# Layer-1 attention scores of a two-layer block: two heads in the two 64-row halves of the array, six part products for eight, masks as 64-row pairs

## The reference

```python
# layer 0, per head
scores = jnp.einsum('bhqd,bhkd->bhqk', q, k) * scale
scores = jnp.where(causal[None, None], scores, -jnp.inf)
scores = scores + head_scales[None, :, None, None] * geo
attn = jax.nn.softmax(scores, axis=-1)
out = jnp.einsum('bhqk,bhkd->bqhd', attn, v).reshape(B, T, C)
return out @ w_out
...
# layer 1, per head; q and k rotated, d = 8
scores = jnp.einsum('bhqd,bhkd->bhqk', q, k) / np.sqrt(HEAD_DIM)
scores = jnp.where(causal, scores, -jnp.inf)
attn = jax.nn.softmax(scores, axis=-1)
out = jnp.einsum('bhqk,bhkd->bhqd', attn, v)
...
h = jax.nn.relu(jnp.einsum('btd,ehd->bteh', x, W1) + b1)
y = jnp.einsum('bteh,edh->bted', h, W2) + b2
return jnp.einsum('bted,bte->btd', y, onehot)
```

## Time and profile before

| | |
|---|---|
| median of 3 runs | 679.21 us (676.43 to 685.65) |
| profiled execution, its time and span | 684.45 us, 682.7 us |
| mean granted TensorE clock | 0.932 |
| busy: TensorE, VectorE, ScalarE, GpSimd | 604.6, 412.7, 338.0, 144.0 us |
| chain that ended last | TensorE 67%, VectorE 19%, DMA 4% |
| part of it S, M, pv | 12%, 9%, 14% |
| S, M matmuls | 576 each, mean 344 and 338 ns |
| exponentials, maxima | 456 each, mean 576 and 656 ns |

### The profile page before, as it was taken

One profiled execution on the slowest core, in us unless ns is written; L12 is line 12 of the kernel. 1 busy time (PEld: TensorE's weight loads), 2 busy tenths in 40 slices (PEclk: granted clock), 3 DMA queues, 4 the chain that ended last, 5 costly groups with the idle time before them and its releaser, 6 DMA issues.

```text
span 682.7 us, 10113 instructions
## 1 busy us (share of the span) xinstructions
PE 604.6 (89%) x3694; PEld 282.8 (41%) x3717; DVE 412.7 (60%) x1031; ACT 338.0 (50%) x621; POOL 144.0 (21%) x180
## 2 busy tenths in 40 slices
PE   5578899958798878889999999999989999899994
PEld 3323233424233224333433344455544555357663
DVE  3586988795603967897778787845657401422313
ACT  4234457634445434546766666645546554633330
POOL 3812212312344022125330202211002001101000
PEclk9889999968658998999999999999999999989998
DMA  4855120000035121031231221030000000000000
GB/s 142 205 175 186 33 75 22 2 1 0 28 75 96 21 43 22 1 64 45 63 49 32 33 45 21 17 48 1 2 0 17 0 2 1 17 0 1 16 1 15
DMA packets 27394, 27.69 MB, mean 41 GB/s; under 512 B 6289, under 2 KB 22545, under 8 KB 27090
## 3 DMA queue, kind: packets, MB, share of 16 engines
q1 hardware_dynamic: 26962, 26.26, 16.2%
q0 software_dynamic: 384, 0.79, 0.5%
HBM read 19.40 MB, written 7.34 MB: 39 GB/s over the span
## 4 chain that ended last, share of the span: by engine, by line
PE 67%; DVE 19%; DMA 4%; ACT 3%; issue 3%; POOL 1%; SPq 1%; DVEq 0%; ACTq 0%; POOLq 0%
PE ps L863 14%; PE ps L846 12%; PE ps L936 10%; DVE mparts L1225 10%; PE ps L823 9%; PE ps L992 8%; PE ps L925 3%; PE ps L919 3%; PE ps L820 2%; ACT pr L1012 2%; PE ps L900 2%; PE ps L874 2%; PE ps L934 2%; DMA qs<-nparts 1%; DVE stats L1135 1%
## 5 line engine op out<-in xcount | busy, mean ns | idle before, releaser
L1012 ACT ACTIVATE pr<-ps 128x512 f32<-128x512 f32 (+1 forms) x456 | 250.6, 576 | 239.3 <-PE ps L846 236.6
L1225 DVE TENSOR_REDUCE mparts<-ps 128x1 f32<-128x512 f32 (+3 forms) x456 | 280.0, 656 | 116.1 <-PE ps L823 114.9
L846 PE MATMUL ps<-qs,ks 99*128 99x512 bf16 (+3 forms) x576 | 174.6, 344 | 12.0 <-ACT pr L1012 6.0
L823 PE MATMUL ps<-ks,qs 96*128 96x512 bf16 (+3 forms) x576 | 170.8, 338 | 15.6 <-DVE mparts L1225 12.7
L740 POOL TENSOR_SCALAR_AFFINE_SELECT pr<-pr 128x512 f32<-128x512 f32 x96 | 60.9, 635 | 370.4 <-ACT pr L1012 370.2
L863 PE MATMUL ps<-pr,vs 128*32 128x512 f32 (+3 forms) x1152 | 131.3, 530 | 0.0
L846 PEld LDWEIGHTS ps<-qs,ks 99*128 99x128 bf16 x576 | 51.0, 100 | 148.6 <-ACT pr L1012 83.9
L823 PEld LDWEIGHTS ps<-ks,qs 96*128 96x128 bf16 x576 | 55.7, 101 | 54.0 <-DVE mparts L1225 21.2
L936 PE MATMUL ps<-w,work 128*128 128x128 f32 x512 | 74.1, 288 | 0.0
L820 PE MATMUL ps<-cmask,identb 128*128 128x128 bf16 (+2 forms) x241 | 58.0, 241 | 17.3 <-DVE mparts L1225 8.9
L1077 ACT ACTIVATE work<-ps,b 128x512 f32<-128x512 f32 x64 | 43.8, 687 | 49.1 <-PE ps L992 48.4
(11 more groups left out here) (115 smaller groups left out, 400.0 us busy)
## 6 DMA issues: line engine op xcount, KB each, us to landing
qs<-scr1q SPq DMA_DIRECT2D x64, 64.0 KB
ks<-scr1k SPq DMA_DIRECT2D x64, 64.0 KB
qs<-scr0q SPq DMA_DIRECT2D x48, 64.0 KB, 2.3
ks<-scr0k SPq DMA_DIRECT2D x36, 64.0 KB, 2.2
scr0q<-parts SPq DMA_DIRECT2D x4, 384.0 KB, 2.9
scr0k<-parts SPq DMA_DIRECT2D x4, 384.0 KB, 3.2
scr1q<-parts SPq DMA_DIRECT2D x4, 384.0 KB, 2.5
scr1k<-parts SPq DMA_DIRECT2D x4, 384.0 KB, 2.5
```

Of the source, the lines that this page charges most:

```text
L823: last = pe.matmul(bank[:, h, :], queries(F, KMAX, h0 + h, i * P, P), ks[0:KMAX, F % SLOTS, h0 + h, 512 * c:512 * c + w], start=not diagon ...
L846: last = pe.matmul(to[:, h, :], ks[0:KEXP, F % SLOTS, h0 + h, j * P:(j + 1) * P], queries(F, KEXP, h0 + h, qb * 512 + lo, n), start=True, ...
L1012: act.activation(pr[:, st % PSLOTS, h0:h0 + nh, 0:STEPS[st][3]], scores_at(F, v), ACT.Exp, scale=GROUPS[F][0].scale).then_inc(exped, 1)
L1225: dve.tensor_reduce(mparts[:, F % SLOTS, h0:h0 + nh, i, c], maxes_at(F, u), AX_X, ALU.max).then_inc(taken, 1)
```

## The change

In layer 1 a head uses six part products like layer 0, 48 rows, 51 with the maximum. Heads 0 and 1 of a group lie in rows 0 to 63 of `qs` and `ks`, heads 2 and 3 in rows 64 to 127; a matmul of a head uses its half alone. Scores go through the heads as 0, 2, 1, 3 and maxima as 2, 0, 3, 1. A unit holds at most two heads, in both layers, so that all its heads lie in one half; the unit of four heads with 128 columns becomes two (38 units a group become 40, in each pass). A mask lies in a head's own half: two matmuls with 64 rows each, of 128 and of 64 columns a head, the second from a mirrored identity and mask (`identx`, `cmaskx`) in the upper half. Loads and row DMAs of layer 1 go by halves: 12 for each of q and k with half the bytes, and six row DMAs for three. The fill of a slot is 1.0 in `ks` (two memsets), at position F-2+0.01 and not F-2+0.1, and loads of groups 4 to 6 wait for it.

```diff
-ATT = [Attention(0, 16, [(0, 0), (0, 1), (1, 0), (1, 1), (0, 2), (2, 0)], 16 ** -0.5),
-       Attention(1, 8, [(0, 0), (0, 1), (1, 0), (1, 1), (0, 2), (2, 0), (1, 2), (2, 1)], 8 ** -0.5)]
...
-KMAX = 96
-KEXP = KMAX + 3
+PRODUCTS = [(0, 0), (0, 1), (1, 0), (1, 1), (0, 2), (2, 0)]
+ATT = [Attention(0, 16, PRODUCTS, 16 ** -0.5), Attention(1, 8, PRODUCTS, 8 ** -0.5)]
+HALF = P // 2
+HEADS = [0, 2, 1, 3]
...
-        nh = min(HG, 512 // n)
-        out += [(s, h, nh) for h in range(0, HG, nh)]
+        nh = min(2, 512 // n)
+        out += [(s, h, nh) for h in HEADS if h % nh == 0]
...
-            nh = min(HG, 512 // w)
-            out += [(i, c, h, nh, w) for h in range(0, HG, nh)]
+            nh = min(2, 512 // w)
+            out += [(i, c, (h + 2) % HG, nh, w) for h in HEADS if h % nh == 0]
...
-    out += [(F - 2 + 0.1, ("zeros", F)) for F in range(ATT[0].groups, ATT[0].groups + SLOTS)]
+    out += [(1.5, ("halves",))]
+    out += [(F - 2 + 0.01, ("ones", F)) for F in range(ATT[0].groups, ATT[0].groups + SLOTS)]
...
-        def queries(F, height, h, lo, n):
-
-            at = HG * 512 * (lo // 512) + h * 512 + lo % 512 if GROUPS[F][0].n == 0 else h * T + lo
-            return qs[0:height, F % SLOTS, at:at + n]
+        def queries(F, more, h, lo, n):
+
+            at = GROUPS[F][0]
+            if at.n == 0:
+                first = HG * 512 * (lo // 512) + h * 512 + lo % 512
+                return qs[0:at.kprod + more, F % SLOTS, first:first + n]
+            base, first = HALF * (h // 2), h % 2 * T + lo
+            return qs[base:base + at.kprod + more, F % SLOTS, first:first + n]
+
+        def keys(F, more, h, lo, n):
+
+            at = GROUPS[F][0]
+            if at.n == 0:
+                return ks[0:at.kprod + more, F % SLOTS, h, lo:lo + n]
+            base = HALF * (h // 2)
+            return ks[base:base + at.kprod + more, F % SLOTS, h % 2, lo:lo + n]
...
-            if F >= SLOTS:
+            if ("ones", F) in NTH:
+                queue.wait_ge(done["ones"], 2 * nth("ones", F))
+            elif F >= SLOTS:
                 queue.wait_ge(scored, (F - SLOTS + 1) * NU)
             cols = (slice(0, T // 2), slice(T // 2, T), slice(0, T))[half]
             for j, pair in enumerate(at.products):
                 src = scr[at.n][k][pair[k]].rearrange("b c t -> (b c) t")[g * at.gw:(g + 1) * at.gw, cols]
+                if at.n == 1:
+                    for pair_of in range(2):
+                        first = HALF * pair_of + j * at.hd
+                        to = (qs, ks)[k][first:first + at.hd, F % SLOTS]
+                        to = to[:, 0:2 * T].rearrange("p (h t) -> p h t", h=2) if k == 0 else to[:, 0:2, :]
+                        heads = src[pair_of * at.gw // 2:(pair_of + 1) * at.gw // 2, :]
+                        queue.dma_start(to, heads.rearrange("(h d) t -> d h t", d=at.hd)).then_inc(qk_in[F % SLOTS][0], 16)
+                    continue
...
+                at = GROUPS[F][0]
                 for p in range(3):
-                    to, src = qs[KMAX + p:KMAX + p + 1, F % SLOTS, cols], nparts[0:n, place, p, :]
-                    if q == 2 and GROUPS[F][0].n == 0:
+                    if at.n == 1:
+                        for pair_of in range(2):
+                            row = HALF * pair_of + at.kprod + p
+                            sp.dma_start(qs[row:row + 1, F % SLOTS, 0:2 * T],
+                                         nparts[2 * TB * pair_of:2 * TB * (pair_of + 1), place, p, :]).then_inc(rows_in, 16)
+                        continue
+                    to, src = qs[at.kprod + p:at.kprod + p + 1, F % SLOTS, cols], nparts[0:n, place, p, :]
+                    if q == 2:
                         to = to.rearrange("a (c x) -> a c x", c=2)
                     sp.dma_start(to, src).then_inc(rows_in if q else rows_first, 16)
...
-            def zeros(F):
+            def halves():
+
+                pool.wait_ge(*before)
+                pool.memset(identx[:, :], 0.0).then_inc(gchain, 1)
+                pool.memset(cmaskx[:, :, :], 0.0).then_inc(gchain, 1)
+                pool.wait_ge(gchain, 5)
+                for first, base in ((0, HALF), (HALF, 0)):
+                    part = slice(first, first + HALF)
+                    pool.affine_select(out=identx[part, :], in_=identx[part, :], compare_op=ALU.not_equal, fill=1.0,
+                                       base=base, pattern=[[-1, P]], channel_multiplier=1).then_inc(done["halves"], 1)
+                    pool.affine_select(out=cmaskx[part, :, :], in_=cmaskx[part, :, :], compare_op=ALU.is_ge, fill=NEG,
+                                       base=base, pattern=[[0, 2], [-1, P]], channel_multiplier=1).then_inc(done["halves"], 1)
+                pool.wait_ge(done["halves"], 4)
+
+            def ones(F):
 
                 pool.wait_ge(scored, (F - SLOTS + 1) * NU)
                 pool.wait_ge(*before)
-                pool.memset(qs[ATT[1].kprod:KMAX, F % SLOTS, :], 0.0).then_inc(done["zeros"], 1)
-                pool.wait_ge(done["zeros"], nth("zeros", F))
+                for first in (32, HALF + 32):
+                    pool.memset(ks[first:first + 32, F % SLOTS, 0:2, :], 1.0).then_inc(done["ones"], 1)
+                pool.wait_ge(done["ones"], 2 * nth("ones", F))
...
-                    if ("zeros", F) in NTH:
-                        pe.wait_ge(done["zeros"], nth("zeros", F))
+                    if F == ATT[0].groups:
+                        pe.wait_ge(done["halves"], 4)
                 if TURN_OF["max", F, u] > MAXN:
                     pe.wait_ge(taken, TURN_OF["max", F, u] - MAXN)
                 diagonal = 512 * c + w == (i + 1) * P
-                if diagonal:
+                if diagonal and GROUPS[F][0].n == 0:
                     pe.matmul(bank[:, :, w - P:w], identb[:, :], cmask[:, 0:nh, :], start=True, stop=False,
                               skip_group_check=True)
+                elif diagonal:
+
+                    own = slice(HALF * (h0 // 2), HALF * (h0 // 2) + HALF)
+                    low, high = ((identb, cmask), (identx, cmaskx))[::-1 if h0 // 2 else 1]
+                    pe.matmul(bank[:, :, w - P:w], low[0][own, :], low[1][own, 0:nh, :], start=True, stop=False,
+                              skip_group_check=True)
+                    pe.matmul(bank[:, :, w - HALF:w], high[0][own, :], high[1][own, 0:nh, HALF:P], start=False, stop=False,
+                              skip_group_check=True)
                 for h in range(nh):
-                    last = pe.matmul(bank[:, h, :], queries(F, KMAX, h0 + h, i * P, P),
-                                     ks[0:KMAX, F % SLOTS, h0 + h, 512 * c:512 * c + w],
+                    last = pe.matmul(bank[:, h, :], queries(F, 0, h0 + h, i * P, P),
+                                     keys(F, 0, h0 + h, 512 * c, w),
                                      start=not diagonal, stop=True, skip_group_check=True)
...
-                        pe.wait_ge(rows_in, 48 * (F + 1))
+                        pe.wait_ge(rows_in, rows_value(F))
...
-                    last = pe.matmul(to[:, h, :], ks[0:KEXP, F % SLOTS, h0 + h, j * P:(j + 1) * P],
-                                     queries(F, KEXP, h0 + h, qb * 512 + lo, n),
+                    last = pe.matmul(to[:, h, :], keys(F, 3, h0 + h, j * P, P),
+                                     queries(F, 3, h0 + h, qb * 512 + lo, n),
```

More of the change, by code:

```diff
@@ L545, in build, with rows_value @@
         block = ctx.enter_context(nc.Block())
[L547 to L550 removed]
+        def queries(F, more, h, lo, n):
[11 more added lines that the diff above has]
+            return ks[base:base + at.kprod + more, F % SLOTS, h % 2, lo:lo + n]
         def loaded(F, i):
[L554 removed]
+            return sum((16, 32, 64)[(G > 0) + (GROUPS[G][0].n == 1)] * len(PRODUCTS) for G in range(F % SLOTS, F + 1, SLOTS)
                        if i == 0 or GROUPS[G][0].n == 0)
+        def rows_value(F):
+            return 48 * (F + 1) + 48 * max(0, F + 1 - ATT[0].groups)
         def maxima_of(F, q):
@@ L749, in _ @@
                     pads(*args)
-                elif kind == "zeros":
-                    zeros(*args)
+                elif kind == "halves":
+                    halves()
+                    before[:] = [done["halves"], 4]
+                    continue
+                elif kind == "ones":
+                    ones(*args)
                 elif kind == "copy_v":
@@ L788, in _ @@
                     continue
-                before[:] = [done[kind], nth(*step)]
+                before[:] = [done[kind], (2 if kind == "ones" else 1) * nth(*step)]
         @block.tensor
```

10 lines of the change are left out of this document (6 added, 4 removed).

## The result

The changed kernel took **721.76 us** (median of 4 runs, 718.62 to 726.81) beside 682.43 us (4 runs) of the kernel before on the same chip: a ratio of 1.061, 95% interval 1.050 to 1.073. Forecast were 674 us, at most 690. The profiled execution took 726.81 us (span 725.1) for 684.45 (span 682.7).

What follows compares the result with a forecast made beforehand. TensorE, busy 89% of the span, was taken to bound the kernel, exponentials pacing groups 6 and 7. Gain -12.7, row DMAs +6.6, units +1.5, loads -1.0 make -5.6 us on 684.45; in proportion 674 us, range 660 to 690.

Steps and rivals of the forecast that it cites:

- The step that failed: Layer-1 score and maximum products: 48 rows for 64 change no matmul's time; the sum gave this no term.
- The fourth rival: Waits at groups' starts grow and TensorE's clock falls, one group taking up to 25 us more: 690 to 699 us; chance 0.06.
- The prediction's own last test: Sign that the forecast is wrong: a layer-1 group shows a granted clock under 1.00.
- The pairs: Layer 1: score and maximum products in opposite halves run together, at most 44 us overlap; 12.7 us gain reaches the time.
- the balance of 5.0 us on TensorE: Groups 6 and 7: TensorE time saved in each, overlap less second mask products and drains at array shape changes.
- The sum: TensorE overlap: counts neighbours in opposite halves in instruction order as pairs, 6.3 us each in groups 6 and 7, a ceiling.
- 2.6 us forecast for the stage: Groups 6 and 7: gain in each, from crossing twelve pv sooner (3.0 us) less drains around the transposes.
- The row DMAs: Starts of layer-1 groups: six for three issue 1.86 us longer, costing 6.6 us over groups 4, 6, 7 and 8.
- Groups 9 to 11: TensorE's balance 0.5, 0.6 and 0.7 us, gain 1.8 us; their length unchanged within 1 us.
- group 10's balance: TensorE in group 10: overlap less masks and drains saves 0.6 us.
- Units: Both layers, at most two heads a unit: splits on ScalarE and VectorE bound at 4.5 us, 1.5 us taken; 480 instructions for 456.
- GpSimd's fills: Starts of groups 2 to 4: paired fills delay a causal fill and its pv, hidden by little, at worst 0.5 us three times.

Runs made afterwards that it cites:

- plain products: Separate kernel of only 512-column products: 64 or 48 rows alone were granted clock 0.50; 128 rows, 96 rows and pairs in both halves kept 1.00.
- one-half kernel: Changed kernel with all four heads of a layer-1 group in rows 0 to 63, so no pairs can run together: 809.21 us, ratio 1.184.
- The two kernels with 64-row halves in all of layer 1: Changed kernel with layer-1 products over all 64 rows of their half, 702.97 us; the same with three row DMAs for six, 705.88 us.
- 64-row kernel: Changed kernel with every layer-1 product over all 64 rows of its half, six row DMAs kept: 702.97 us, ratio 1.039.

## Why the prediction was wrong

**The step that failed** is the sentence "Two products fewer (48 rows for 64) change no matmul's time; rows don't count, columns do." Rows count for no single product, but for the clock at which all of them run. Before, S had 99 rows and M 96; after, 51 and 48, and since S and M are seldom both ready, mostly one half works alone. The fourth rival came nearest, a falling clock, but it blamed waits at a group's start, put 690 to 699 us on it and gave it 0.06. The runs put rows in the waits' place for the most part: by ratios, 13 or 16 rows more in each product bring back 1.061 - 1.039, about 15 us, with the waits for the row DMAs still there; the falls in groups 6 and 7 of the changed kernel come with TensorE busy for 3.56 to 3.79 of the 4 us before; and in plain products rows alone make the difference. Waits keep a share: the falls at the start of group 4 and at that of group 7 of the one-half kernel follow one, and there few rows only explain that the clock stayed away (54.9 us busy without a gap at 0.50). The argument against that rival ("group 7 already starts with a wait and keeps 1.00") held for products of 96 and 99 rows and said nothing of fewer. The prediction's own last test, a layer-1 group under 1.00, is what came.

**The pairs.** Right in kind (6 ns), oversized: the balance of 5.0 us on TensorE in groups 6 and 7 was 3.1 to 3.7 at full clock (30.9 against 27.2 to 27.8 busy). The sum counted every neighbour in opposite halves as a pair; of the 96 S and M of a stage 15 to 17 start within 40 ns of the one before. Of the 2.6 us forecast for the stage 1.7 and 1.9 came, once clock and row DMAs were mended.

**The row DMAs.** Issue +1.9 us, as forecast. Cost 1.5 us in each of groups 6 and 7 (31.1 and 31.0 against 29.6 and 29.5), forecast 0.9 and 1.9: right in sum. In the changed kernel itself group 6 waits 1.55 us for them, and in groups 7 and 8 they hide behind the slow clock.

**Groups 9 to 11** were to stay within 1 us. Groups 9 and 10 did, at 1.00; that overlap, masks and drains balance in them, as the sum has it, was not taken apart, and group 10's balance is 0.3 by the sum's own terms, not 0.6. Group 11 missed, with 3.4 us more: 3.4 us at the lower level cost at most half of that, and the rest is open. The two kernels with 64-row halves in all of layer 1 took 45.6 and 47.1 us from the first S to the end of the last, the kernel before and those with group 11 in the old layout 40.8.

**Units** cost between nothing and 4.5 us in all, which cannot tell 0 from 1.5; in groups 6 and 7 they cost nothing. The exponentials and the maxima are 480 each, as forecast.

**GpSimd's fills** were said to be hidden but for 0.5 us. They are not in group 3. In the 64-row kernel, whose group 3 took 57.9 us, the rows of GpSimd, ScalarE and TensorE make one chain:

```profile
193.24 3.65 POOL L776 MEMSET ks<- 32x2048 bf16 x2
196.97 1.26 POOL L819 TENSOR_TENSOR work<-work 128x512 f32<-128x512 f32 x1
198.26 0.62 ACT L1103 CAST parts<-work 128x512 bf16<-128x512 f32 x1 [5.40 <-POOL work L819]
198.79 0.59 ACT L1078 ACTIVATE pr<-ps 128x512 f32<-128x512 f32 x1
199.43 0.50 PE L912 MATMUL ps<-qs,ks 99*128 99x384 bf16 x1 [4.69 <-ACT pr L1078]
...
201.74 1.94 PE L929 MATMUL ps<-pr,vs 128*32 128x512 f32 x8
```

The fills delay a product of the rotation, ScalarE's cast waits 5.40 us for it, an exponential stands behind the cast on the same engine, and S waits 4.69 us. I had followed the fill to the causal mask and not to ScalarE. The clock fell at 197.4, within that wait, and pv runs at half of it (1.94 us). The changed kernel has the same wait of ScalarE (5.2 us), but there the clock had been low since 175.9, TensorE was late with its own work, and S waits only 0.22 and 1.38 us. So groups 3 and 4 can lose by this chain and by the clock, and the two were not taken apart: of their 22.9 us, 64 rows give back 11.1; the rest stays open. So does why group 4 is granted 0.78 in one 64-row kernel and 0.67 in the other. Group 2, nearly the same instructions in all these kernels, took from 63.6 to 70.3 us at 0.84 and 0.75, so a few microseconds of any total here are luck of that kind.

## What to carry to other kernels

Price a narrower contraction twice: by its columns, and by what it may do to the clock; look at the granted clock of the stage before and after, and do not count on it where fewer rows work at once. Row halves pay where both halves have work ready; with one alone, zeros up to 96 rows cost no time in the products here and kept the clock, but filling them cost about 8 us in one group. Follow every added instruction of a side engine to the next in-order engine that waits for it, not only to the consumer one has in mind.
